# Transposed x in three places instead of two, block 2's free half ahead of the first selections, and one indirect gather fewer issued ahead

## The chip, the cores and the metric

The kernel runs on one core of one Trainium2 chip. The metric is the device time of one execution in microseconds (us); lower is better. The core has five engines that run beside each other and meet at semaphores: TensorE (PE: matmuls; PEld: its weight loads), VectorE (DVE), ScalarE (ACT), GpSimd (POOL) and SyncE (SP, which here only issues DMAs). SBUF is the on-chip memory, PSUM the banks that TensorE writes.

## The reference, cut to what matters

Two LoRA layers follow each other on x of shape (64, 32, 512), each with one adapter per batch row, chosen by an id:

```
x = x + (x W^T + bias + (x A[id0]^T) Bw[id0]^T)     # 32 adapters, rank 16
x = x + (x B1[id1]^T) A1[id1]^T                     # 8 adapters, rank 16
```

The products are in float32. The kernel splits each operand into a rounded high part and the remaining low part and adds three products (high-high, high-low, low-high), the list `HALVES` in the code.

## The kernel before, in words

The 2048 rows of x are cut in 16 blocks of 128 rows; a block holds four batches (`NB`), so four adapter ids per layer. Everything is unrolled, and each engine has its order written out by hand.

**Set-up.** TensorE transposes W (`w_fill`), the adapter tables (`bw`, `a0` to `a3`) and the first three blocks of x (`x_fill`, L409). It also multiplies tables with each other (`c1_part`, and fill "g", L478 to L482), so that the second layer can act on the first layer's input. ScalarE copies each PSUM result to SBUF as the high part, VectorE subtracts for the low part. The rows by which the second factor is applied (`by_rank`, 640 rows of 644 floats) are written to DRAM by SP, ending with `row_ends` (L223). After that GpSimd can gather.

**Per block k.**
- `x_turn(k)` (VectorE, from block 3 on) puts the transposed x in PSUM bank 7. `xt_high(k)` (ScalarE) and `xt_low(k)` (VectorE) bring it to `xt`, which has two places, used in turn. `xt_high(k)` waits until block k-2's matmuls have read theirs.
- `select(k, layer)` (ScalarE, L566) copies the four batches' adapters of a layer into the D columns of `wd`, beside the columns of W. There are two sets of D columns, so it waits for block k-2 too (`u_filled`).
- `base(k, chunks, halves)` (TensorE, L383) multiplies x by W, in two halves of the output columns. One half takes the D columns along (384 columns a matmul), the other is free of them (256 columns). Each chunk of 128 inputs is three matmuls per half. For even k, half 0 is the free one; for odd k, half 1.
- `turn_u(k)`, `own_u(k)` (VectorE) mask the adapters' output per batch and add one gathered column; `add_gh(k)` (TensorE, L429) adds what the second layer needs of the first layer's update, from `g_sel`, which GpSimd makes in `g_select(k)` from the gathered rows; `u_high(k)` and `u_low(k)` bring that to SBUF.
- `gather(k)` (GpSimd, L316) issues the indirect DMA of 128 rows by id into one of four buffers. `up_high(k)` (ScalarE) and `up_low(k)` (GpSimd) split them in high and low. `up(k)` (TensorE, L435) applies them; `finish(k)` (VectorE) adds the bias; SP stores.

**The order around the change.** GpSimd issues gathers 0, 1 and 2, and then repeats: g_select(k), up_low(k), gather(k+3). SP issues the x loads in groups (`X_GROUPS`): group 3 (block 3) and group 4 (blocks 4 and 5) one straight after the other behind `row_ends`; group 5 (blocks 6 and 7) behind the store of block 0.

TensorE goes from set-up into the blocks in this order: the free half of block 1, the transpose of block 2's x, then block 0's other half: the first two chunks without D columns, a wait for the first selections, `down` (L401) for the D columns of these two chunks alone, and the last two chunks with D columns. Then the D half of block 1 and the free half of block 2, add_gh(0), and so on:

```
            base(0, [0, 1], halves=[1], with_d=False, group_check=False)
            wait_d(0)
            down(0, [0, 1])
            base(0, [2, 3], halves=[1], group_check=False)
```

## Time and profile before

| | |
|---|---|
| time, median of 3 runs | 98.52 us (98.05 to 98.83) |
| the profiled execution's own time | 97.92 us |
| its span in the profile | 95.8 us (2.1 us lie outside) |
| TensorE busy | 91.5 us, 96% of the span |
| VectorE, ScalarE, GpSimd busy | 68%, 61%, 61% |
| granted TensorE clock | full over the span (mean 0.997) |
| one block, from an add_gh in the chain of waits to the next (44.38 to 48.81 us) | 4.4 us |

The times of the table's first line come from executions without the profiler; all rows below come from the one profiled execution and are times from its span's start. Matmuls overlap, so a duration in a timeline row is longer than what the matmul adds to a row of them; the chain of waits counts each stretch once. An engine's idle time before an instruction stands in square brackets, with what ended it.

### The profile page before, as it was taken

To read this page: it belongs to the slowest core of one execution; us is meant where nothing else is said; L and a number is where in the kernel's file an instruction comes from. 1 tells how busy PE (TensorE), PEld (TensorE's weight loads), DVE (VectorE), ACT (ScalarE), POOL (GpSimd) and SP (SyncE) were. 2 spreads that over 40 slices of the span, in tenths; PEclk is the share of its full clock that TensorE was granted. 3 is DMA by queue.
4 is the path that set the end of the run, shared out by engine and by line. 5 is a ranking of instruction groups with operands and counts; after the bars stand their busy time and mean duration, and the time that the engine had idled before them with its cause. 6 is when DMAs were issued, how large, how long until landed. Compare 5 with 4: busy or idle time off the path is not lost.

```text
span 95.8 us, 2305 instructions
## 1 busy us (share of the span) xinstructions
PE 91.5 (96%) x662; PEld 90.0 (94%) x662; DVE 64.8 (68%) x120; ACT 58.7 (61%) x189; POOL 58.0 (61%) x126
## 2 busy tenths in 40 slices
PE   5999999999999999999999999999999999999980
PEld 5899999999899998999999999999999999999970
DVE  4499799227076468959587877768595868786460
ACT  0074598874588796748494948567584949480210
POOL 6504008850568999999576584959585766808500
PEclk9999999999999999999999999999999999999998
DMA  2999998968896289989996499992836354520205
GB/s 40 312 347 387 374 403 262 281 156 214 215 224 223 53 250 238 310 249 235 203 290 218 70 319 209 238 269 91 228 44 229 34 213 54 200 110 0 110 0 219
DMA packets 16335, 19.45 MB, mean 203 GB/s; under 512 B 1444, under 2 KB 11556, under 8 KB 16164
## 3 DMA queue, kind: packets, MB, share of 16 engines
q1 hardware_dynamic: 15040, 14.04, 50.1%
q0 software_dynamic: 1280, 5.28, 22.1%
q8 instruction: 5, 0.08, 0.4%
q14 instruction: 6, 0.05, 0.3%
q10 hardware_dynamic: 4, 0.00, 0.0%
HBM read 13.47 MB, written 5.84 MB: 202 GB/s over the span
## 4 chain that ended last, share of the span: by engine, by line
PE 90%; DVE 4%; ACT 2%; issue 1%; DVEq 0%; ACTq 0%
PE psum L394 55%; PE psum L440 11%; PE psum L432 4%; PE psum L362 4%; PE psum L480 4%; PE psum L378 4%; PE psum L370 3%; DVE table_rounded L640 3%; PE psum L466 2%; PE psum L414 1%; PE psum L405 1%; PE psum L448 1%; DVE y L679 1%; ACT row_ends L558 1%; ACT table_rounded L558 1%
## 5 line engine op out<-in xcount | busy, mean ns | idle before, releaser
L394 PE MATMUL psum<-wd,xt 128*128 128x256 f32 (+1 forms) x384 | 62.3, 310 | 0.0
L394 PEld LDWEIGHTS psum<-wd,xt 128*128 128x128 f32 x384 | 56.1, 188 | 0.0
L558 ACT ACTIVATE wd<-table_rounded 128x128 fp32r x128 | 27.7, 297 | 14.7 <-PE psum L394 12.5
L339 POOL TENSOR_TENSOR up_rows<-gathered_rows,up_rows 128x512 fp32r<-128x512 f32 x16 | 20.6, 1289 | 14.0 <-ACT up_rows L558 14.0
L322 POOL DMA_INDIRECT gathered_rows<-by_rank,rows x16 | 15.9, 996 | 6.3 <-DMA by_rank<-row_ends 3.8
L640 DVE TENSOR_TENSOR xt<-psum,xt 128x512 fp32r<-128x512 f32 x16 | 11.1, 691 | 6.6 <-ACT xt L558 5.9
L647 DVE STREAM_TRANSPOSE psum<-x_squares 128x512 f32<-128x512 f32 x13 | 14.4, 1110 | 0.0
L440 PE MATMUL psum<-up_rows,u_sel 128*128 128x256 f32 x96 | 14.2, 284 | 0.0
L440 PEld LDWEIGHTS psum<-up_rows,u_sel 128*128 128x128 f32 x96 | 12.8, 190 | 0.2
L659 DVE STREAM_TRANSPOSE psum<-psum 128x128 f32<-128x128 f32 x16 | 5.3, 330 | 11.2 <-PE psum L394 7.8
L332 POOL TENSOR_TENSOR g_sel<-gathered_rows,batch_mask 128x16 f32<-128x16 f32 x64 | 12.1, 227 | 0.9 <-DMA gathered_rows<-by_rank,rows 0.7
L558 ACT ACTIVATE xt<-psum 128x512 fp32r<-128x512 f32 x16 | 9.6, 597 | 4.4 <-DVE psum L647 1.8
L679 DVE TENSOR_TENSOR y<-psum,bias_all 128x512 f32<-128x512 f32 x15 | 10.4, 692 | 1.1 <-PE psum L440 0.5
L558 ACT ACTIVATE up_rows<-gathered_rows 128x512 fp32r<-128x512 f32 x16 | 10.0, 623 | 0.0
L558 ACT ACTIVATE u_sel<-psum 128x128 fp32r<-128x128 f32 x16 | 4.2, 262 | 5.8 <-PE psum L432 5.8
L432 PE MATMUL psum<-u_own,g_sel 128*128 128x128 f32 x32 | 6.3, 279 | 0.1
L640 DVE TENSOR_TENSOR u_sel<-psum,u_sel 128x128 fp32r<-128x128 f32 x16 | 4.6, 288 | 2.3 <-ACT u_sel L558 2.3
L666 DVE SCALAR_TENSOR_TENSOR u_own<-psum,gathered_rows,batch_mask 128x128 f32<-128x128 f32 x16 | 5.6, 348 | 0.5
L432 PEld LDWEIGHTS psum<-u_own,g_sel 128*128 128x128 f32 x32 | 5.3, 188 | 0.5 <-issue 0.5
L281 POOL COPY a_by_rank<-a_rows 128x1024 f32<-128x1024 f32 x1 | 2.0, 2010 | 5.3 <-DMA a_rows<-in_L_cond_A 5.3
L362 PE MATMUL psum<-warm 128*128 128x128 f32 x16 | 3.9, 425 | 1.1 <-DVE warm L683 1.1
L362 PEld LDWEIGHTS psum<-warm 128*128 128x128 f32 x16 | 3.6, 330 | 1.1 <-DVE warm L683 1.1
(60 smaller groups left out, 72.1 us busy)
## 6 DMA issues: line engine op xcount, KB each, us to landing
out<-y SPq DMA_DIRECT2D x15, 256.0 KB
x_squares<-in_x SPq DMA_DIRECT2D x8, 256.0 KB
w_rows<-in_L_cond_base_weight SPq DMA_DIRECT2D x4, 256.0 KB, 4.0
bw_rows<-in_L_cond_lora_B_w SPq DMA_DIRECT2D x1, 1024.0 KB, 7.0
a_rows<-in_L_cond_lora_A_w SPq DMA_DIRECT2D x1, 1024.0 KB, 9.2
by_rank<-bw_by_rank SPq DMA_DIRECT2D x4, 256.0 KB
x_squares<-in_x SPq DMA_DIRECT2D x8, 128.0 KB
x_rows<-in_x SPq DMA_DIRECT2D x3, 256.0 KB, 9.3
```

Of the source, the lines that this page charges most:

```text
L322: nc.gpsimd.indirect_dma_start(out=gathered_rows[:, k % GATHERS, :], out_offset=None, in_=by_rank_dram[:, :], in_offset=bass.IndirectOffse ...
L332: last = nc.gpsimd.tensor_tensor(out=g_sel[:, k % 2, b, L1, :], in0=gathered_rows[:, k % GATHERS, bass.ds(n1[b] * R + G_COL, R)], in1=batc ...
L339: nc.gpsimd.tensor_tensor(out=up_rows[:, k % 2, LO, :], in0=gathered_rows[:, k % GATHERS, 0:D], in1=up_rows[:, k % 2, HI, :], op=ALU.subtr ...
L362: nc.tensor.matmul(XT[:, 0:P], warm[:, :], warm[:, :], start=True, stop=True)
L394: last = nc.tensor.matmul(bank_of(k, half)[:, start:end], xt[:, k % 2, c, x_part, :], wd[:, w_part, c, col:col + end - start], start=(c == ...
L432: nc.tensor.matmul(u_now, g_sel[:, k % 2, :, :, :], u_own[:, :], start=True, stop=True).then_inc(gh_filled, 1)
L440: last = nc.tensor.matmul(products(k)[:, half, :], u_sel[:, k % 2, u_part, :], up_rows[:, k % 2, r_part, half * HALF:(half + 1) * HALF], s ...
L558: return nc.scalar.activation(dst, src, ACT.Copy)
L640: return nc.vector.tensor_tensor(out=dst, in0=whole, in1=high, op=ALU.subtract)
L647: nc.vector.transpose(out=XT.rearrange("p (c b s) -> p b c s", c=C, b=NB), in_=x_squares[:, k * NB:(k + 1) * NB, :].rearrange("p b (i c) - ...
L666: nc.vector.scalar_tensor_tensor(out=u_own[:, :], in0=u_blocks, scalar=gathered_rows[:, k % GATHERS, BB_COL:BB_COL + 1], in1=batch_mask[:, ...
L679: nc.vector.tensor_tensor(out=y[:, k % SLOTS, :].rearrange("p (h n) -> p h n", h=2), in0=products(k), in1=bias_all[:, :].rearrange("p (h n ...
```

## The change

- `xt` gets three places (`X_SLOTS`). `xt_high(k)` then waits for block k-3.
- The transpose of block 2's x stands straight behind the table product "g" on TensorE, ahead of the 16 transposes of the `a` table. `xt_high(2)` moves ahead of the four `table0` copies on ScalarE, `xt_low(2)` ahead of the four `table0` subtractions on VectorE.
- TensorE does the free half of block 2 straight behind that of block 1, then waits for the first selections, then does the whole D half of block 0 in one piece. `down` and the form of `base` without D columns go.
- ScalarE: `up_high(0)` stands ahead of `select(2, L1)`, `xt_high(3)` behind `u_high(0)`. `select` loads its ids ahead of its wait.
- VectorE: `own_u(0)` stands ahead of `x_turn(3)`.
- GpSimd: gathers 0 and 1 are issued ahead, and then gather(k+2) behind up_low(k).
- SP: the load of x group 4 waits until gather 0 has landed.

```
+X_SLOTS = 3
+ROWS_AHEAD = 2
-        xt = sb("xt", [P, 2, C, 2, P], F32R)
+        xt = sb("xt", [P, X_SLOTS, C, 2, P], F32R)
@@ SP
             for k in range(NBLK - 1):
+                if k == 0:
+
+                    sp.wait_ge(gathered[0], 16)
                 if k in (0, 1, 3, 6):
                     load_x(4 + (0, 1, 3, 6).index(k))
@@ GpSimd
-            gather(0)
-            gather(1)
-            gather(2)
+            for k in range(ROWS_AHEAD):
+                gather(k)
             for k in range(NBLK):
                 g_select(k)
                 up_low(k)
-                if k + 3 < NBLK:
-                    gather(k + 3)
+                if k + ROWS_AHEAD < NBLK:
+                    gather(k + ROWS_AHEAD)
@@ TensorE
             last.then_inc(filled, 1)
+            x_fill(2)
             pe.wait_ge(a_in, 16)
...
             base(1, range(C), halves=[1])
-            x_fill(2)
+            wait_x(2)
+            wait_drained(pe, "a0")
+            base(2, range(C), halves=[0])
+
+
             wait_drained(pe, "c1")
-            base(0, [0, 1], halves=[1], with_d=False, group_check=False)
             wait_d(0)
-            down(0, [0, 1])
-            base(0, [2, 3], halves=[1], group_check=False)
+            base(0, range(C), halves=[1])
             wait_drained(pe, "a3")
             wait_d(1)
             base(1, range(C), halves=[0])
-            wait_x(2)
-            base(2, range(C), halves=[0])
             add_gh(0)
@@ ScalarE
+                if k >= X_SLOTS:
+                    act.wait_ge(u_filled, k - X_SLOTS + 1)
+                copy(xt[:, k % X_SLOTS, :, HI, :], chunked(XT)).then_inc(xt_hi_ready, 1)
...
+            xt_high(2)
             for g in range(4):
...
-            xt_high(2)
             select(2, L0)
+            up_high(0)
             select(2, L1)
-            up_high(0)
+            u_high(0)
             xt_high(3)
-            u_high(0)
             select(3, L0)
@@ VectorE
+            xt_low(2)
             for g in range(4):
...
             turn_u(0)
-            xt_low(2)
+            own_u(0)
             x_turn(3)
-            own_u(0)
+            u_low(0)
             xt_low(3)
-            u_low(0)
             turn_u(1)
```

TensorE's instructions before, from the table product "g" (L480) to the second add_gh (L432). The L394 rows are `base`, L405 is `down`, L414 the transpose of block 2's x, L440 `up`:

```order
L480 MATMUL psum<-b_cols,bw_cols 128x128 x16
L487 MATMUL psum<-ident,a_rows 128x128 x16
L394 MATMUL psum<-wd,xt 128x256 x12
L414 MATMUL psum<-ident,x_rows 128x128 x4
L394 MATMUL psum<-wd,xt 128x256 x6
L405 MATMUL psum<-wd,xt 128x128 x6
L394 MATMUL psum<-wd,xt 128x384 x18
L394 MATMUL psum<-wd,xt 128x256 x12
L432 MATMUL psum<-u_own,g_sel 128x128
L394 MATMUL psum<-wd,xt 128x384 x6
L440 MATMUL psum<-up_rows,u_sel 128x256 x6
L394 MATMUL psum<-wd,xt 128x384 x6
```

The same stretch after the change (L397 is `base` now, L408 the transpose, L426 add_gh, L434 `up`):

```order
L474 MATMUL psum<-b_cols,bw_cols 128x128 x16
L408 MATMUL psum<-ident,x_rows 128x128 x4
L482 MATMUL psum<-ident,a_rows 128x128 x16
L397 MATMUL psum<-wd,xt 128x256 x24
L397 MATMUL psum<-wd,xt 128x384 x24
L426 MATMUL psum<-u_own,g_sel 128x128
L397 MATMUL psum<-wd,xt 128x384 x6
L434 MATMUL psum<-up_rows,u_sel 128x256 x6
L397 MATMUL psum<-wd,xt 128x384 x6
L426 MATMUL psum<-u_own,g_sel 128x128
```

The four transposes moved up by 28 matmuls, the six matmuls of 128 columns are gone, and six of 256 columns became six of 384. The 24 of 256 columns all stand ahead of the first one that needs a selection.

ScalarE before, from the last copy of select(2, L0) on: the ids' load and four copies of select(2, L1), up_high(0), xt_high(3), u_high(0), and the ids' load of select(3, L0):

```order
L241 TENSOR_LOAD ids
L558 ISA
L558 ACTIVATE wd<-table_rounded 128x8x16
L558 ISA
L558 ACTIVATE wd<-table_rounded 128x8x16
L558 ISA
L558 ACTIVATE wd<-table_rounded 128x8x16
L558 ISA
L558 ACTIVATE wd<-table_rounded 128x8x16
L558 ACTIVATE up_rows<-gathered_rows 128x512
L558 ACTIVATE xt<-psum 128x4x128
L558 ACTIVATE u_sel<-psum 128x128
```

The same stretch after the change:

```order
L553 ACTIVATE up_rows<-gathered_rows 128x512
L246 TENSOR_LOAD ids
L553 ISA
L553 ACTIVATE wd<-table_rounded 128x8x16
L553 ISA
L553 ACTIVATE wd<-table_rounded 128x8x16
L553 ISA
L553 ACTIVATE wd<-table_rounded 128x8x16
L553 ISA
L553 ACTIVATE wd<-table_rounded 128x8x16
L553 ACTIVATE u_sel<-psum 128x128
L553 ACTIVATE xt<-psum 128x4x128
```

up_high(0), which waits for gather 0, now stands ahead of the four copies of select(2, L1), and u_high(0) ahead of xt_high(3).

## Rows read from the trace of the kernel before

**Rows 1.** The page: busy time of each engine, and the chain that ended last.

```profile
PE 91.5 (96%) x662; PEld 90.0 (94%) x662; DVE 64.8 (68%) x120; ACT 58.7 (61%) x189; POOL 58.0 (61%) x126
PE 90%; DVE 4%; ACT 2%; issue 1%; DVEq 0%; ACTq 0%
```

**Rows 2.** The chain of waits in order of time: start us, us, what.

```profile
20.93 2.50 DVE table_rounded L640 x4
...
24.21 0.30 ACT wd L558
...
25.44 4.65 PE psum L394 x30
...
33.17 0.33 PE psum L432 x2
...
36.19 0.46 PE psum L432 x2
...
39.99 0.22 PE psum L432 x2
```

**Rows 3.** Timeline, TensorE: start us, us, engine line operation out<-in xcount [idle before <-releaser].

```profile
21.46 1.68 PE L394 MATMUL psum<-wd,xt 128*128 128x256 f32 x12
22.97 0.65 PE L414 MATMUL psum<-ident,x_rows 128*128 128x128 f32 x4
23.38 0.96 PE L394 MATMUL psum<-wd,xt 128*128 128x256 f32 x6
24.55 0.89 PE L405 MATMUL psum<-wd,xt 128*128 128x128 f32 x6 [0.21 <-ACT wd L558]
25.27 4.81 PE L394 MATMUL psum<-wd,xt 128*128 128x384 f32 x30
```

**Rows 4.** Timeline, ScalarE.

```profile
26.64 0.60 ACT L558 ACTIVATE xt<-psum 128x512 fp32r<-128x512 f32 x1 [1.34 <-issue]
27.14 1.96 ACT L558 ACTIVATE wd<-table_rounded 128x128 fp32r x8
29.00 0.62 ACT L558 ACTIVATE up_rows<-gathered_rows 128x512 fp32r<-128x512 f32 x1
...
32.13 0.90 ACT L558 ACTIVATE wd<-table_rounded 128x128 fp32r x4
```

**Rows 5.** Timeline, GpSimd: gathers 0, 3 and 4, and what stands between them.

```profile
24.63 1.16 POOL L322 DMA_INDIRECT gathered_rows<-by_rank,rows  x1 [3.77 <-DMA by_rank<-row_ends]
...
28.96 0.77 POOL L332 TENSOR_TENSOR g_sel<-gathered_rows,batch_mask 128x16 f32<-128x16 f32 x4 [0.66 <-DMA gathered_rows<-by_rank,rows]
29.69 1.29 POOL L339 TENSOR_TENSOR up_rows<-gathered_rows,up_rows 128x512 fp32r<-128x512 f32 x1
...
31.13 0.99 POOL L322 DMA_INDIRECT gathered_rows<-by_rank,rows  x1
...
34.28 0.99 POOL L322 DMA_INDIRECT gathered_rows<-by_rank,rows  x1 [0.16 <-POOL up_rows L339]
...
38.45 0.75 POOL L332 TENSOR_TENSOR g_sel<-gathered_rows,batch_mask 128x16 f32<-128x16 f32 x4
```

**Rows 6.** DMA queues, 31.0 to 34.5 us: packets, MB, share of 16 engines (q0: gathers).

```profile
q0 software_dynamic: 81, 0.33, 34.1%
```

**Rows 7.** DMA queues, 35.0 to 39.1 us (q1: what SP issues, q0: gathers).

```profile
q1 hardware_dynamic: 1089, 0.60, 60.1%
q0 software_dynamic: 79, 0.33, 35.5%
```

**Rows 8.** DMA queues, 35.0 to 37.25 us.

```profile
q1 hardware_dynamic: 794, 0.40, 75.4%
q0 software_dynamic: 13, 0.07, 31.3%
```

**Rows 9.** Timeline, SP: the store of block 0, then x group 5.

```profile
32.87 0.36 SPq L230 DMA_DIRECT2D out<-y  x1
33.27 2.76 SPq L194 DMA_DIRECT2D x_squares<-in_x  x4
```

More of the change, by code:

```diff
@@ L381, in c1_part, with base @@
                     last.then_inc(filled, 1)
-            def base(k, chunks, with_d=True, halves=range(2), group_check=True):
+            def base(k, chunks, halves=range(2)):
                 left = W_LEFT[k % 2]
                 regions = [(left, left + HALF, P), (left, left + HALF, P + HALF)]
-                if with_d:
-                    at_half, at = U_AT[k % 2]
-                    start = min(at, left)
-                    regions[at_half] = (start, start + HALF + P, min(D_AT[k % 2], P + at_half * HALF))
+                at_half, at = U_AT[k % 2]
+                start = min(at, left)
+                regions[at_half] = (start, start + HALF + P, min(D_AT[k % 2], P + at_half * HALF))
                 for c in chunks:
@@ L393, in base @@
                             start, end, col = regions[half]
-                            last = nc.tensor.matmul(bank_of(k, half)[:, start:end], xt[:, k % 2, c, x_part, :],
+                            last = nc.tensor.matmul(bank_of(k, half)[:, start:end], xt[:, k % X_SLOTS, c, x_part, :],
                                                     wd[:, w_part, c, col:col + end - start],
-                                                    start=(c == 0 and n == 0), stop=(c == C - 1 and n == 2),
-                                                    skip_group_check=not group_check)
-                if with_d and C - 1 in chunks and U_AT[k % 2][0] in halves:
+                                                    start=(c == 0 and n == 0), stop=(c == C - 1 and n == 2))
+                if C - 1 in chunks and U_AT[k % 2][0] in halves:
                     last.then_inc(u_filled, 1)
-            def down(k, chunks):
-                half, at = U_AT[k % 2]
-                for c in chunks:
-                    for x_part, d_part in HALVES:
-                        nc.tensor.matmul(bank_of(k, half)[:, at:at + P], xt[:, k % 2, c, x_part, :],
-                                         wd[:, d_part, c, D_AT[k % 2]:D_AT[k % 2] + P],
-                                         start=False, stop=True, skip_group_check=True)
             def x_fill(k):
@@ L561, in xt_high, with select @@
                 act.wait_ge(xt_filled, k + 1)
+                if k >= X_SLOTS:
+                    act.wait_ge(u_filled, k - X_SLOTS + 1)
+                copy(xt[:, k % X_SLOTS, :, HI, :], chunked(XT)).then_inc(xt_hi_ready, 1)
+            def select(k, layer, n=None):
+                ready, table = ((sel0_ready, table0_rounded), (sel1_ready, table1_rounded))[layer]
+                n = n or adapters_of(act, k, layer)
                 if k >= 2:
                     act.wait_ge(u_filled, k - 1)
-                copy(xt[:, k % 2, :, HI, :], chunked(XT)).then_inc(xt_hi_ready, 1)
-            def select(k, layer, n=None):
-                ready, table = ((sel0_ready, table0_rounded), (sel1_ready, table1_rounded))[layer]
-                if k >= 2:
-                    act.wait_ge(u_filled, k - 1)
-                n = n or adapters_of(act, k, layer)
                 for b in range(NB):
@@ L652, in xt_low @@
                 dve.wait_ge(xt_hi_ready, k + 1)
-                low(xt[:, k % 2, :, LO, :], chunked(XT), xt[:, k % 2, :, HI, :]).then_inc(xt_lo_ready, 1)
+                low(xt[:, k % X_SLOTS, :, LO, :], chunked(XT), xt[:, k % X_SLOTS, :, HI, :]).then_inc(xt_lo_ready, 1)
             def turn_u(k):
```

## The prediction

> **What bounds the kernel now.** I read the page first. TensorE is busy 96% of the span and makes 90% of the chain that ended last [rows 1]. So only two things can move the time: work that TensorE no longer does, and moments at which it waits. I read the chain in order of time next. From 40 us on it is TensorE alone, in blocks of 4.4 us, and nothing in the change takes an instruction from it there. All that can change lies between 20 and 40 us. There the chain leaves TensorE once: the VectorE's four table subtractions and ScalarE's first selection, which ends at 24.51 us [rows 2]. TensorE's timeline shows the price, 0.21 us idle ahead of the 128-column matmuls [rows 3]. The second limit is hidden in "busy": GpSimd. From the landing of gather 0 (28.96 us) it runs g_select, up_low and gather issue in turns of 34.28 - 31.13 = 3.15 us [rows 5], against 33.17 to 36.19 us between TensorE's second and third add_gh [rows 2]. The two run in step until 36 us. Only at the fourth add_gh (39.99 us) does TensorE come after GpSimd's g_sel (38.45 + 0.75 = 39.20 us) with room to spare [rows 2, 5]. What the change is worth is read at that fourth add_gh, because everything behind it is TensorE's own pace.
>
> **TensorE's own work.** Twelve matmuls of 256 columns start 22.97 - 21.46 = 1.51 us before their successor [rows 3], so 0.126 us each. The 4.65 us of the chain are 18 of 384 columns and 12 of 256 [rows 2], so (4.65 - 1.51) / 18 = 0.174 us for one of 384. The six of 128 columns take 25.27 - 24.55 = 0.72 us [rows 3], 0.12 each: a narrow matmul costs nearly as much as one of 256. Removed are six of those (0.72) and six of 256 (0.76), added are six of 384 (1.04): 0.44 us less. The four transposes take 23.38 - 22.97 = 0.41 us [rows 3] and are only moved, so the free half of block 1 starts at 21.46 + 0.41 = 21.87, and ends at 23.38. Block 2's free half fills the time to 24.89.
>
> **The tables come later.** xt_high(2) and xt_low(2) now stand ahead of the table work. Before, four subtractions take 2.50 us [rows 2], 0.62 for one more of the same size in a row of them. ScalarE's copies are 0.60 [rows 4] and half hidden. So the first selection ends at 24.51 + 0.62 = 25.13 us, and TensorE, ready at 24.89, waits until about 25.17: the old wait of 0.21 stays a wait of about 0.28. Then 24 matmuls of 384 columns take 4.18 us, and TensorE is at add_gh(0) at 29.35, where the chain of before had it at 25.44 + 4.65 = 30.09 [rows 2]. That is 0.74 us gained, if the gathered rows are there.
>
> **The first gather.** It was issued at 24.63 us and its rows were used at 28.96 [rows 5], 4.33 us. Gather 3, issued at 31.13 with next to nothing beside it, had its 80 packets through at about 34.5 [rows 6]. With 0.4 to 0.5 us from last packet to use, that is 3.8 us; the issue itself is 0.99 instead of 1.16 [rows 5]. So the rows of gather 0 should be there at 28.4 to 28.5: 0.5 us gained. Bounds: nothing (28.96), or some 0.8 us if company cost it more than the quiet gather 3 shows. But here ScalarE caps it: up_high(0) stands behind select(2, L0), which can only start when block 0's D half is through at 25.17 + 12 x 0.174 = 27.26, plus 0.33 to the signal's use (before, block 0's last matmul went in by 25.27 + 6 x 0.174 = 26.31 and xt_high(2), which waited for it, began at 26.64 [rows 3, 4]), plus 0.95 (half of the 1.96 us in rows 4): 28.5. Landing earlier than that gains nothing.
>
> A rule that says otherwise: the Trainium skill, "DMA: Bandwidth & Descriptors", section "Anatomy of one DMA", gives a gpsimd-issued DMA about 2.0 us plus bytes by 436 GB/s, which is an estimated 2.8 us for 330 KB. Rows 5 and 6 show about 3.8 alone and 4.33 in company, so the measured numbers stay in the sum; by the page every gather would be early, and the result would be that of the first rival.
>
> **A new wait on ScalarE.** Behind add_gh(0), TensorE does block 2's D half, which needs select(2, L1). Before, that was done at 29.10 [rows 4]. Now it stands behind up_high(0): 28.5 + 0.5 for that copy's turn + 0.9 for the four copies [rows 4] = 29.95. TensorE is through with add_gh(0) at 29.6 and waits 0.4 us. Then 6 x 0.174 = 1.04, up(0) with six of 256 columns 0.76, again 1.04: add_gh(1) at 32.85, 0.3 ahead of the old 33.17 [rows 2]. On GpSimd, up_low(0) ends at 29.07 + 0.1 + 1.29 = 30.5, gather 2 is issued at 30.6, g_select(1) is done at 32.4. On VectorE, x_turn(3) now follows own_u(0), from 28.8 to 29.9, and u_low(0) comes at 30.2, so it costs nothing. add_gh(2) then waits for GpSimd's next turn, 0.45 us ahead of before: 36.19 - 0.45 = 35.75. Gather 2 must be there at 34.9. Issued at 30.6 beside the tail of x group 4 (loaded from 28.4 on), it takes what gather 0 took in like company, 4.33: 34.93. It just fits.
>
> **What is late next: gather 3.** It used to be issued at 31.13, in the quiet; now it is issued behind up_low(1), at 34.28 - 0.45 = 33.8, which is where gather 4 stood. The store of block 0 and x group 5 run from 32.87 to 36.03 [rows 9]. Gather 4 got 13 of its 80 packets by 37.25 us while SP's queue moved 794 [rows 8], and all of them only by 39.1 [rows 7]: 4.8 us from its issue, 5.3 with the landing. Nobody missed it, since g_select(4) comes a turn behind g_select(3), at 41.6. Gather 3 is wanted at 38.45 [rows 5]. I take 5.1 us, between this and the 3.8 us of a quiet one, and near the first, since x group 5 still runs but the store of block 1, a turn later, hardly meets it: there at 38.9. g_select(3) ends 0.77 later and add_gh(3) follows at 39.8 to 39.9, against 39.99 before. Bounds: at 3.8 us it is there at 37.6, no wait, and the whole 0.45 us stays; at 6.0 (an estimate: 5.3 and twice the 0.35 us by which it stands closer behind x group 5 than gather 4 did) it comes at 39.8, and add_gh(3) at 40.7, 0.7 us later than before.
>
> The skill, same page, section "Queues, rings and completion order", has each DMA engine go round robin between queues at packet borders; then a 5 KB gather packet would only wait for one small packet of 512 bytes, and gather 3 would hardly suffer. Rows 8 disagree: 13 gather packets in the time of 794 others. The rows decide.
>
> Later gathers have more room. In the steady stretch a turn is 4.4 us, so from the end of up_low(k) to up_high(k+2), the first use, there are 8.8 - 0.62 - 1.29 - 0.16 = 6.7 us [rows 4, 5], more than 5.3. The third place of xt and the ids' loads ahead of the wait free ScalarE where it isn't late: nothing. x group 4 is issued from 28.4 to 31.2 (2.76 us [rows 9]) and first wanted by x_turn(4), behind finish(1) and so behind up(1), not before 35 us; gather 0, in company, was there 4.3 us from its issue: nothing.
>
> **The sum.** -0.74 at add_gh(0); +0.4 for select(2, L1) leaves -0.3; GpSimd's turn sets -0.45 at add_gh(2); +0.35 for gather 3 leaves -0.1 us. Against the profiled execution's 97.92 us that is 97.8. The median of the runs is 0.60 above that execution, so I forecast 98.4.
>
> **The rivals.**
> - All gathers land in time (gather 3 in about 4 us). For it: rows 6. Against: rows 8. Gain 0.45 us, 98.1.
> - TensorE alone sets the pace: table, selections and gathers all early. The most there is: 0.44 us of work, 0.21 idle and some 0.25 of waits from 30.09 to 36.19 (6.1 us, in which 18 matmuls of 384 columns, 18 of 256 and two add_gh of 0.22 make 5.85): 0.9 us, 97.6. Against: two of the waits are moved, not removed.
> - The other side, gather 0 gains nothing: its 4.33 us are its own, and x group 4 (SP's queue was nearly through when it began) never hurt it. Then up_high(0) is at 29.0 as before, select(2, L1) at 30.5, TensorE waits 0.9 us, gather 3 is issued at 34.28 and lands at 39.5, add_gh(3) at 40.45: +0.5, 99.0.
> - The other side, dearer: gather 3 meets more of x group 5 than gather 4 did, being issued 0.65 instead of 1.0 us behind it. It decides from a landing later than 39.1. At 40.1 it costs 1.0 us, since add_gh(3), and with it ScalarE's selections for block 5 behind up_high(3), all move: 99.5.
>
> **Chances.** The forecast (within 0.3 us of it) 0.42, all gathers in time 0.22, TensorE alone 0.10, gather 0 gains nothing 0.15, gather 3 dearer 0.11. The range 97.7 to 99.2 leaves out most of the second and the last. About 1% (1 us) is what a measurement of this kernel tells from no change: faster 0.12, within 0.77, slower 0.11.
>
> **What would show it.** Right: no 128-column matmuls of `down`; add_gh(0) near 29.4 and a stop of about 0.4 us behind it that ScalarE's wd ends; gather 0 used at 28.4 to 28.5; GpSimd idle for about 0.9 us ahead of g_select(3), with the gather as releaser; add_gh(3) at 39.8 to 39.9; span 95.7. Wrong: gather 3 used at once (then 98.1), gather 0 still at 28.9, a stop of TensorE behind 40 us, or a span off by more than 0.7 us.

## The result, and the profile after

| | before | after |
|---|---|---|
| median of 22 runs | 98.53 us (97.92 to 99.51) | 99.68 us (98.14 to 101.07) |
| the profiled execution's own time | 97.92 us | 100.11 us |
| its span | 95.8 us | 98.0 us |
| a second profiled execution | | 99.14 us, span 97.0 |

The changed kernel is slower: the ratio of the executions that lie within 1.5% of their kernel's fastest is 1.006 [1.0033, 1.0088], which leaves out 11 of the changed kernel's 22 and one of before's, so it understates. The medians of all runs stand at 99.68 / 98.53 = 1.012. The changed kernel's best run, 98.14 us, is a run like before's; its others spread over 3 us where before's spread over 1.6. The forecast was 98.4 us and the range ended at 99.2.

The page's lines on engines and chain, after, against [rows 1]:

```profile
PE 91.9 (94%) x656; PEld 90.2 (92%) x656; DVE 64.8 (66%) x120; ACT 59.4 (61%) x189; POOL 57.9 (59%) x126
PE 59%; DMA 24%; issue 5%; SPq 3%; POOL 3%; DVE 1%; ACT 1%; POOLq 0%; DVEq 0%
```

TensorE has six instructions less and about the busy time that it had. But it makes 59% of the chain where it made 90%; DMA, which doesn't stand among the engines of [rows 1]'s chain, makes 24%. The chain in order of time says which transfers (start us, us, what):

```profile
4.55 9.85 DMA x_rows<-in_x
...
21.00 3.75 DMA by_rank<-row_ends
...
25.62 4.01 DMA gathered_rows<-by_rank,rows
...
35.12 5.48 DMA gathered_rows<-by_rank,rows
...
41.68 0.46 PE psum L426 x2
```

The first, 9.85 us, is the load of the first x in the set-up, and has nothing to do with the blocks. The other three make 13.24 us. Where [rows 2] has VectorE's tables, then TensorE throughout, the chain now runs over the landing of `row_ends`, gather 0 (issued at 25.62 us) and gather 3 (at 35.12 us), and from `row_ends` on comes to TensorE only at the fourth add_gh, 41.68 us. TensorE's timeline, after, against [rows 3]:

```profile
22.43 3.09 PE L397 MATMUL psum<-wd,xt 128*128 128x256 f32 x24
25.84 4.47 PE L397 MATMUL psum<-wd,xt 128*128 128x384 f32 x24 [0.32 <-ACT wd L553]
30.73 0.46 PE L426 MATMUL psum<-u_own,g_sel 128*128 128x128 f32 x2 [0.42 <-POOL g_sel L337]
...
41.68 0.46 PE L426 MATMUL psum<-u_own,g_sel 128*128 128x128 f32 x2 [0.86 <-POOL g_sel L337]
```

`down` is gone, and two stops at add_gh have come, both ended by GpSimd's g_sel. GpSimd's timeline, after, against [rows 5], shows why g_sel is late:

```profile
25.62 1.16 POOL L327 DMA_INDIRECT gathered_rows<-by_rank,rows  x1 [4.25 <-DMA by_rank<-row_ends]
...
29.83 0.76 POOL L337 TENSOR_TENSOR g_sel<-gathered_rows,batch_mask 128x16 f32<-128x16 f32 x4 [1.80 <-DMA gathered_rows<-by_rank,rows]
...
35.12 0.99 POOL L327 DMA_INDIRECT gathered_rows<-by_rank,rows  x1 [0.16 <-issue]
...
40.78 0.76 POOL L337 TENSOR_TENSOR g_sel<-gathered_rows,batch_mask 128x16 f32<-128x16 f32 x4 [1.50 <-DMA gathered_rows<-by_rank,rows]
...
42.93 0.99 POOL L327 DMA_INDIRECT gathered_rows<-by_rank,rows  x1
...
49.77 0.76 POOL L337 TENSOR_TENSOR g_sel<-gathered_rows,batch_mask 128x16 f32<-128x16 f32 x4 [2.68 <-DMA gathered_rows<-by_rank,rows]
```

GpSimd waits 1.50 us for gather 3 and 2.68 us for gather 5 (issued at 42.93). Before, it waited for neither: g_select(3) has no idle time in [rows 5], and g_select(5) none in the same timeline.

**One clock for all profiles.** The same program reaches the blocks some tenths earlier or later: in the changed kernel's profile TensorE stood 0.5 us for the first load of x, in the set-up. So times below are also told from the start of ScalarE's copy into `row_ends` at the end of the table product "g". ScalarE's timeline of before, and then of the changed kernel:

```profile
19.81 0.60 ACT L558 ACTIVATE row_ends<-psum 128x512 f32<-128x512 f32 x1 [0.90 <-PE psum L480]
```

```profile
20.30 0.60 ACT L553 ACTIVATE row_ends<-psum 128x512 f32<-128x512 f32 x1 [0.91 <-PE psum L474]
```

Each figure is the start of a TensorE timeline row less the start of that copy; the last column is the span's end less it.

| from the copy, us | add_gh(0) | add_gh(1) | add_gh(2) | add_gh(3) | add_gh(5) | end |
|---|---|---|---|---|---|---|
| before | 10.11 | 13.22 | 16.38 | 20.02 | 28.83 | 75.99 |
| changed | 10.43 | 13.82 | 16.73 | 21.38 | 30.37 | 77.70 |
| changed, second profile | 10.33 | 13.73 | 16.65 | 20.85 | 30.13 | 77.44 |

The 2.2 us between the two spans are then 0.49 of a late start, which has nothing to do with the blocks, some 0.35 up to the third add_gh, 1.0 more at the fourth, and 0.35 more up to the end. The second profile has no late start: 0.27 at the third, 0.56 more at the fourth, 0.62 behind it.

### The profile page after: what moved, and what is told of

It reads as the page before. It is cut to its first block, busy times and chain, and to the rows that moved or that the text cites. A ratio compares the mean times of both kernels' runs of the same rounds, so it can differ in the third digit from the quotient of the medians.

```text
span 98.0 us, 2293 instructions
## 1 busy us (share of the span) xinstructions
PE 91.9 (94%) x656; PEld 90.2 (92%) x656; DVE 64.8 (66%) x120; ACT 59.4 (61%) x189; POOL 57.9 (59%) x126
## 4 chain that ended last, share of the span: by engine, by line
PE 59%; DMA 24%; issue 5%; SPq 3%; POOL 3%; DVE 1%; ACT 1%; POOLq 0%; DVEq 0%
PE psum L397 43%; DMA x_rows<-in_x 10%; DMA gathered_rows<-by_rank,rows 10%; PE psum L434 9%; DMA by_rank<-row_ends 4%; PE psum L474 4%; PE psum L426 3%; POOL g_sel L337 2%; SPq L202 2%; PE psum L408 1%; POOL up_rows L344 1%; DVE y L674 1%; ACT row_ends L553 1%; SPq L205 0%; SPq L204 0%
## 5 line engine op out<-in xcount | busy, mean ns | idle before, releaser
L397 PE MATMUL psum<-wd,xt 128*128 128x256 f32 (+1 forms) x384 | 62.5, 311 | 0.4 <-ACT wd L553 0.3
L397 PEld LDWEIGHTS psum<-wd,xt 128*128 128x128 f32 x384 | 56.4, 188 | 0.7 <-issue 0.7
L434 PE MATMUL psum<-up_rows,u_sel 128*128 128x256 f32 x96 | 14.1, 283 | 0.0
L434 PEld LDWEIGHTS psum<-up_rows,u_sel 128*128 128x128 f32 x96 | 12.9, 190 | 0.0
L426 PE MATMUL psum<-u_own,g_sel 128*128 128x128 f32 x32 | 6.4, 283 | 1.3 <-POOL g_sel L337 1.3
L426 PEld LDWEIGHTS psum<-u_own,g_sel 128*128 128x128 f32 x32 | 5.2, 188 | 2.1 <-DVE u_own L661 1.8
```

The lines of the kernel that those rows point to most:

```text
L397: last = nc.tensor.matmul(bank_of(k, half)[:, start:end], xt[:, k % X_SLOTS, c, x_part, :], wd[:, w_part, c, col:col + end - start], start ...
L426: nc.tensor.matmul(u_now, g_sel[:, k % 2, :, :, :], u_own[:, :], start=True, stop=True).then_inc(gh_filled, 1)
L434: last = nc.tensor.matmul(products(k)[:, half, :], u_sel[:, k % 2, u_part, :], up_rows[:, k % 2, r_part, half * HALF:(half + 1) * HALF], s ...
```

## The experiments

Theory A, from the two profiles: the loss is gather 3, and behind it gather 5, because two gathers ahead put them beside x groups 5 and 6. Theory B: it is the new order in front (the free half, the table a copy later, up_high(0) early). Theory C: it is SP's wait for gather 0.

### Three ahead in the changed kernel

```
-ROWS_AHEAD = 2
+ROWS_AHEAD = 3
```

> The changed kernel with three gathers issued ahead again (gather(k+3) behind up_low(k)); all else as changed. Theory A (gather 3, now issued where gather 4 was, lands late and holds the fourth add_gh): the stop of TensorE ahead of the fourth add_gh (0.86 us) goes, and the one at the sixth with it; time 1.0 to 2.0 us below the changed kernel, ratio to before 0.993 to 1.000. Theory B (the new order on TensorE and ScalarE between 20 and 32 us is what costs): the time stays at 1.006 or more. Theory C (x group 4, held back until gather 0 has landed, is what meets the gathers): partly better, 1.002 to 1.006.

98.3 us against 98.45, ratio 1.0006 [0.9973, 1.0039]. The loss is gone with this one number, as theory A said. From the copy, add_gh(0) is at 9.95, add_gh(3) at 19.93, the end at 75.90. GpSimd, in this kernel's timeline:

```profile
34.26 0.99 POOL L327 DMA_INDIRECT gathered_rows<-by_rank,rows  x1 [0.16 <-POOL up_rows L344]
...
38.45 0.75 POOL L337 TENSOR_TENSOR g_sel<-gathered_rows,batch_mask 128x16 f32<-128x16 f32 x4
```

These are the rows of before almost to the hundredth [rows 5]. But nothing is gained either.

### The changed kernel without SP's wait

```
             for k in range(NBLK - 1):
-                if k == 0:
-                    sp.wait_ge(gathered[0], 16)
```

> The changed kernel without SP's wait for gather 0 ahead of x group 4. Theory A: gather 3 still lands about 5.5 us behind its issue, since its company is x group 5 and the stores; ratio to before 1.005 to 1.015, as the changed kernel. Theory C: the ratio falls to 1.000 or below. If the wait does what it is for (a quiet first gather), gather 0 is used 0.3 us or more later from its issue than the 4.0 us of the changed kernel.

99.89 us, ratio 1.013 [1.0077, 1.0183]. The wait isn't the loss; theory C falls. Gather 3 took from 35.17 us 5.31 us in the chain, add_gh(3) stands at 20.81.

### Two ahead in the kernel before

```
             gather(1)
-            gather(2)
...
-                if k + 3 < NBLK:
-                    gather(k + 3)
+                if k + 2 < NBLK:
+                    gather(k + 2)
```

> The kernel before with one edit: gathers 0 and 1 ahead, then gather(k+2) behind up_low(k). Theory A: this part alone makes it slower than before, by 0.8 to 2 us, ratio 1.008 to 1.02, with TensorE waiting for g_sel ahead of the fourth add_gh. Theories B and C: within 0.3 us of before, ratio 0.997 to 1.003.

100.18 us, ratio 1.0156 [1.0106, 1.0205]: the largest loss of all, with nothing else changed. The chain of this kernel:

```profile
34.69 5.78 DMA gathered_rows<-by_rank,rows
...
42.80 6.93 DMA gathered_rows<-by_rank,rows
...
50.81 0.46 PE psum L431 x2
```

Gather 3 takes 5.8 us to its first use, gather 5 takes 6.9, and TensorE waits at the fourth and the sixth add_gh (21.33 and 30.59 from the copy). Theory A holds for the cause: two ahead costs 0.6 to 1.6%, in either order of the rest.

### The new order alone

The changed kernel with ROWS_AHEAD = 3 and without SP's wait: both edits above together.

> The changed kernel with both DMA edits undone (three gathers ahead, no wait of SP): only the third place of xt and the new order on TensorE, ScalarE and VectorE remain. Theory A: a gain, ratio 0.993 to 0.999, the 0.45 us of the forecast or less. Theory B: 1.003 or more.

98.4 us, ratio 1.0009 [0.9981, 1.0037]. The order neither costs nor gains that these runs could tell; the expected gain (0.993 to 0.999) didn't come. Theory B falls as a cause of the loss; what became of the 0.44 us of TensorE's work is the question of the next runs. This run and the second differ by ROWS_AHEAD alone, and their intervals lie apart (1.0009 and 1.013).

### Three dummy matmuls, in both orders

Is the order's gain lost because TensorE then only waits longer for gather 0? Three matmuls of zeros stand ahead of add_gh(0), into columns that nobody has written yet and that are written anew later. The first kernel has the new order alone, the second is before:

```
+            for _ in range(3):
+                nc.tensor.matmul(bank_of(2, 1)[:, 0:P], warm[:, :], warm[:, :], start=True, stop=True)
             add_gh(0)
```

> The order-only kernel with three matmuls of zeros, 0.22 us each, put ahead of add_gh(0); their result is overwritten. Theory D' says that TensorE has 0.5 us or more to spare there: the time moves by less than 0.3 us, ratio to before 0.999 to 1.004. If TensorE's work sets the pace: +0.67 us, 1.007.

> The kernel before with the same three matmuls ahead of add_gh(0). There TensorE arrives just as g_sel is ready: the time rises by 0.4 to 0.7 us, ratio 1.004 to 1.008. If it stays within 0.1%, TensorE had room there too, and the place is set by something else.

New order: 98.55 us, 1.0012 [0.9981, 1.0042]. Before: 98.8 us, 1.0023 [0.9994, 1.0052], where 1.004 to 1.008 was expected. Neither is clear of noise, so what follows is read from profiles. TensorE's timeline of the new order with the dummies:

```profile
30.09 0.83 PE L500 MATMUL psum<-warm 128*128 128x128 f32 x6
30.75 0.39 PE L423 MATMUL psum<-u_own,g_sel 128*128 128x128 f32 x2
```

The six rows of the dummies take 30.75 - 30.09 = 0.66 us. In the kernel before, add_gh(0) moves from 10.11 to 10.77, the full 0.66, and add_gh(3) from 20.02 to 20.22: on the way some 0.46 us of more work is swallowed. In the new order the profiles compare less simply, because gather 0's issue moved as well. Against the new order alone (gather 0 issued 5.10 us behind the copy) add_gh(0) goes from 10.32 to 10.51 and add_gh(3) from 20.27 to 20.16, but with the dummies gather 0 was issued at 4.62. Against three ahead in the changed kernel (issued at 4.89) they are 0.56 and 0.23 us later. That the new order swallows more than the old one isn't shown.

What sets the pace is read from GpSimd and TensorE. GpSimd's g_sel(2) and TensorE's add_gh(2) and add_gh(3) in the new order alone:

```profile
35.79 0.76 POOL L334 TENSOR_TENSOR g_sel<-gathered_rows,batch_mask 128x16 f32<-128x16 f32 x4
```

```profile
36.69 0.46 PE L423 MATMUL psum<-u_own,g_sel 128*128 128x128 f32 x2
...
40.34 0.38 PE L423 MATMUL psum<-u_own,g_sel 128*128 128x128 f32 x2
```

add_gh(2) starts 36.69 - 35.79 - 0.76 = 0.14 us behind the end of g_sel(2), and add_gh(3) 3.65 us behind that. It is 0.14 with three ahead in the changed kernel and 0.15 before. So in both orders GpSimd's turns, counted from gather 0's landing, set the third add_gh, and while they do, work taken from TensorE ahead of add_gh(0) can't pay. The next two runs tried to shorten those turns.

### A fourth gather ahead, to free GpSimd's first turn

```
-            for k in range(ROWS_AHEAD):
+            for k in range(GATHERS):
                 gather(k)
...
-                if k + ROWS_AHEAD < NBLK:
+                if k >= 1 and k + ROWS_AHEAD < NBLK:
```

> The new order without the DMA edits (as the order-only run), and all four gathers issued ahead, so that GpSimd's first turn has no gather in it. Theory D (in the order-only run the gain of the new order was lost at GpSimd's turns of 3.15 us from the landing of gather 0): g_select(1) comes 1.1 us sooner behind g_select(0), the second and third add_gh 0.3 to 0.6 us sooner, ratio to before 0.993 to 0.998. Theory E (TensorE's own waits for the selections ate the gain): 0.999 to 1.003.

> The kernel before with all four gathers issued ahead, GpSimd's first turn without a gather. Theory D: TensorE's waits at the second and third add_gh, 0.25 us in all, go: ratio 0.996 to 0.999. If the fourth gather delays g_select(0) by more than 0.4 us: 1.000 or above.

The fences show the edit in the new order; in the kernel before it is the same. The new order: 98.96 us, 1.0039 [1.0008, 1.0071], a small loss where a gain was expected. Before: 98.74 us, 1.0026 [0.9994, 1.0058]. GpSimd in the first of them:

```profile
28.95 0.95 POOL L324 DMA_INDIRECT gathered_rows<-by_rank,rows  x1 [0.30 <-issue]
29.92 0.75 POOL L334 TENSOR_TENSOR g_sel<-gathered_rows,batch_mask 128x16 f32<-128x16 f32 x4
```

The fourth issue ends only when gather 0 has long landed (ScalarE uses it 4.12 us from its issue, GpSimd 4.94), so what the first turn saves, its start loses; add_gh(0) waits 0.96 us for it and add_gh(3) stands at 20.70.

### Filling the wait for gather 0 with block 2's D half

The new order alone; TensorE takes the first two chunks of block 2's D half ahead of add_gh(0), and ScalarE makes their selection ahead of up_high(0):

```
-            add_gh(0)
             wait_d(2)
             base(2, [0, 1], halves=[1])
+            add_gh(0)
+            base(2, [2, 3], halves=[1])
             up(0)
-            base(2, [2, 3], halves=[1])
             add_gh(1)
...
             select(2, L0)
+            select(2, L1)
             up_high(0)
-            select(2, L1)
             u_high(0)
```

> The order-only kernel with block 2's D half put where TensorE waits: its first two chunks ahead of add_gh(0), its last two ahead of up(0), and select(2, L1) ahead of up_high(0) for that. Theory D' (what was gained ahead of add_gh(0) is lost waiting for gather 0, since nothing else may run there): TensorE has work through the wait, ratio to before 0.993 to 0.998. Theory F (ScalarE's selections and copies are then what is late): 0.999 to 1.006, with waits behind ScalarE's up_rows or wd.

99.52 us, 1.01 [1.0056, 1.0144]: 1% lost, more than either theory had. ScalarE and then GpSimd, in this kernel's timeline:

```profile
30.42 0.61 ACT L550 ACTIVATE up_rows<-gathered_rows 128x512 fp32r<-128x512 f32 x1
...
31.11 1.28 POOL L341 TENSOR_TENSOR up_rows<-gathered_rows,up_rows 128x512 fp32r<-128x512 f32 x1 [1.07 <-ACT up_rows L550]
```

The selection's place was taken from up_high(0), GpSimd stood idle 1.07 us for it in its first turn, and every later turn came later by that: add_gh(3) at 20.95.

### Only gather 3 late, only the later ones late (before)

```
                 up_low(k)
-                if k + 3 < NBLK:
+                if k == 1:
+                    gather(3)
+                if k >= 1 and k + 3 < NBLK:
                     gather(k + 3)
```

> The kernel before with gather 3 alone issued later: behind up_low(1) with gather 4 right behind it; from then on as before. Theory A in its narrow form (gather 3 alone makes the loss): TensorE waits for g_sel 1 us or more ahead of the fourth add_gh, ratio 1.008 to 1.018, no stop at the sixth. If the later gathers of the two-ahead order make the loss: 0.998 to 1.005.

99.34 us, ratio 1.0086 [1.0058, 1.0113]. But this run doesn't isolate the landing: with gathers 3 and 4 issued one behind the other, GpSimd's turn is longer, and in the profile the stop is at the third add_gh, a turn ahead of gather 3's use:

```profile
37.07 0.46 PE L434 MATMUL psum<-u_own,g_sel 128*128 128x128 f32 x2 [0.90 <-POOL g_sel L332]
```

So its 0.86% bounds nothing of gather 3's transfer alone. The other half:

```
                 up_low(k)
-                if k + 3 < NBLK:
-                    gather(k + 3)
+                if k < 2:
+                    gather(k + 3)
+                if 3 <= k < NBLK - 2:
+                    gather(k + 2)
```

> The kernel before with gathers 3 and 4 issued as before and the later ones as after the change: none behind up_low(2), then gather(k+2) behind up_low(k) from k = 3 on. Theory A in two parts (gather 3 makes 0.85 us of the two-ahead order's 1.5, the gathers beside x group 6 the rest): ratio 1.003 to 1.009, with GpSimd or TensorE waiting for gather 5 ahead of the sixth add_gh. If only gather 3 counts: 0.998 to 1.002.

98.64 us, ratio 1.0022 [0.9993, 1.0052]. GpSimd waits 1.58 us at 46.91 and 2.35 us at 52.40 for gathers, and no add_gh of TensorE waits (28.85 from the copy at the sixth, as before). So here late gathers in the steady stretch cost nothing that can be measured. In the kernels with two ahead, which come there behind a late gather 3, the profiles show 0.1 to 0.5 us lost from the fourth to the sixth add_gh; that the debt makes the difference isn't shown by a run of its own.

### x group 5 one block later

The direct test of theory A's mechanism: two gathers ahead stay, and only the company of gather 3 goes.

```
-                if k in (0, 1, 3, 6):
-                    load_x(4 + (0, 1, 3, 6).index(k))
+                if k in (0, 2, 3, 6):
+                    load_x(4 + (0, 2, 3, 6).index(k))
```

> The changed kernel with x group 5 (blocks 6 and 7) issued behind the store of block 1 instead of block 0. Theory A1 (gather 3 is late because of its company, x group 5 and the stores): gather 3 is used about 4.2 us behind its issue instead of 5.5, no wait of TensorE ahead of the fourth add_gh, ratio to before 0.998 to 1.004. Theory A2 (a gather behind others takes 5.5 us whatever is beside it): 5.3 us or more again and 1.008 to 1.015.

> The run with x group 5 later once more, for a second profile. Its first profile showed gather 3 quiet (used within 4.2 us) and gather 5 at 7.4 us, and a time of 98.3, while other executions took 99.2 to 101.0. Theory A1: in a profile of a longer execution the difference is a stop of TensorE of 1 us or more at the fifth to seventh add_gh, behind a gather beside x group 6.

Six runs: 99.74 us (98.29 to 100.99), ratio 1.0122 [1.0072, 1.0171], where 0.998 to 1.004 was expected; the three fastest alone stand at 1.006. The profile was that of the fastest of them, 98.29 us. A second profile has 100.08 us. In both, gather 3 is out of the way. GpSimd and the queues in the first:

```profile
33.99 0.99 POOL L327 DMA_INDIRECT gathered_rows<-by_rank,rows  x1 [0.15 <-issue]
...
38.18 0.75 POOL L337 TENSOR_TENSOR g_sel<-gathered_rows,batch_mask 128x16 f32<-128x16 f32 x4
```

DMA queues, same kernel, 34.0 to 37.4 us (packets, MB, share of 16 engines):

```profile
q0 software_dynamic: 84, 0.33, 35.6%
q1 hardware_dynamic: 160, 0.29, 22.7%
```

No wait ahead of g_select(3), and add_gh(3) at 19.81 from the copy, and at 19.80 in the second profile: the only kernels that beat before's 20.02 there by as much as 0.2. Then gather 5 meets x group 6, which holds four blocks where group 5 holds two. The second profile's chain, and its queues from 41.3 to 49.7 us:

```profile
41.34 8.33 DMA gathered_rows<-by_rank,rows
...
50.75 0.46 PE psum L426 x2
```

```profile
q1 hardware_dynamic: 2915, 1.64, 94.9%
q0 software_dynamic: 87, 0.33, 19.3%
```

In the fastest run gather 5 took 7.42 us in the chain and cost TensorE 0.3 us; in the second profile 8.33 and 1.2 us, a stop of the size that was expected there. So the same program differs from run to run by how gather and x load meet. That isn't all of the 1.8 us between the two spans (96.2 and 98.0), though: 1.04 of them is the start (the copy at 19.74 and at 20.78), and 0.76 lies behind it.

### Both x groups a block later

```
-                if k in (0, 1, 3, 6):
-                    load_x(4 + (0, 1, 3, 6).index(k))
+                if k in (0, 2, 4, 6):
+                    load_x(4 + (0, 2, 4, 6).index(k))
```

> The changed kernel with x group 5 issued behind the store of block 1 and x group 6 behind that of block 3 (before: blocks 0 and 2). Theory A1 (two gathers ahead fail because gathers 3 and 5 meet x groups 5 and 6): gathers 3 and 5 are used 4 to 5 us behind their issue, TensorE doesn't stop at the fourth or sixth add_gh, ratio to before 0.999 to 1.004. Theory A3 (moving the loads only moves the meeting to another gather): 1.008 or more, with a stop at another add_gh.

98.82 us (97.59 to 99.94), before 98.58, ratio 0.9991 [0.9948, 1.0034]; the medians of all runs stand at 1.002. Two ahead, and the loss is no longer to be seen. The queues while gather 3 is on its way, 35.25 to 38.5 us, and then GpSimd from gather 5 on:

```profile
q0 software_dynamic: 82, 0.33, 34.8%
q1 hardware_dynamic: 135, 0.24, 19.8%
```

```profile
41.67 0.99 POOL L327 DMA_INDIRECT gathered_rows<-by_rank,rows  x1 [0.16 <-POOL up_rows L344]
...
46.52 0.75 POOL L337 TENSOR_TENSOR g_sel<-gathered_rows,batch_mask 128x16 f32<-128x16 f32 x4
```

Neither gather is waited for. GpSimd now waits for gather 4 instead (0.68 us) and for gather 7 (1.61 us), but no add_gh behind the first one stops. (In this profile add_gh(3) is at 20.98 and the end at 76.98 all the same: gather 0 was issued 5.88 us behind the copy, 1.06 later than before, and add_gh(0) stands at 10.79. So the profile shows where the waits went, and the runs that the loss went.) So the cost of two ahead is the company that SP gives the gathers, and not the distance by itself.

### Three ahead and both groups later

The same with ROWS_AHEAD = 3, to see whether the two together beat before.

> The changed kernel with three gathers ahead and x groups 5 and 6 a block later each: both cures at once. Theory A1: with three ahead the gathers had room enough beside the loads, so the second cure adds nothing: ratio to before 0.997 to 1.002. If loads beside gathers cost something even with three ahead: 0.993 to 0.997, a version better than both.

99.75 us, ratio 1.0074 [1.0032, 1.0116], and 1.013 by the medians of all runs: neither of the two outcomes that were expected. At the sixth add_gh it is the earliest of all profiles (28.71 from the copy), and then VectorE waits for x group 6 itself, block 8's transpose:

```profile
55.31 1.10 DVE L642 STREAM_TRANSPOSE psum<-x_squares 128x512 f32<-128x512 f32 x1 [1.64 <-DMA x_squares<-in_x]
```

From the seventh add_gh to the eighth it is 58.83 - 53.64 = 5.19 us for before's 4.43, and these 0.76 us are the whole of what this profile's end, 76.65, lies behind that of three ahead alone, 75.90. Behind the store of block 3 the x load had too little room: it is issued from 45.29 us on and used at 55.31. With two ahead it was issued from 45.74 and used at 54.05 without a wait. Why the load took longer here I can't say; the intervals (to 1.0034 there, from 1.0032 here) just touch.

### The changed kernel, a second profile

> The changed kernel once more, for a second profile. Theory A: whatever its time, the distance from the end of the table product to the fourth add_gh goes with gather 3: 21.6 us in the first profile, with gather 3 used 5.5 us behind its issue; if it is used within 4.8 us this time, the distance is under 20.9.

99.14 us, 1 us less than the first profile. Its chain:

```profile
34.30 5.03 DMA gathered_rows<-by_rank,rows
...
41.66 6.94 DMA gathered_rows<-by_rank,rows
...
49.69 0.46 PE psum L426 x2
```

Gather 3 takes 5.03 us here (5.48 in the first), more than the 4.8 us that the expectation set as its condition, and add_gh(3) is at 20.85 (21.38); gather 5 takes 6.94 and comes into the chain at the sixth add_gh. Of the 1.0 us between the two spans, 0.74 is the start (19.56 for 20.30) and only 0.26 lies behind the copy. But both lose 1.45 to 1.7 us there against before, so the loss is no matter of one unlucky profile.

## Why the prediction was wrong, point by point

**What TensorE does: right.** The rows of 128 columns are gone. From the first matmul of 384 columns to add_gh(0), where nothing is waited for between them (group 5 one block later), it is 9.85 - 5.55 = 4.30 us from the copy's clock, for a forecast of 4.18.

**The tables come later: right, and 0.18 us short.** First selection's matmuls expected 25.17 - 19.81 = 5.36 us behind the copy; 5.54 and 5.55 in the profiles of the changed kernel, and 5.54 to 5.63 in all others with the new order whose row shows it. The stop was 0.32 us for the forecast's 0.28.

**"The rows of gather 0 should be there at 28.4 to 28.5: 0.5 us gained": wrong, and the first step that failed.** That is 8.69 us behind the copy for up_high(0). It was at 9.35 and 9.25 in the changed kernel, 9.19 before. SP's wait did keep x group 4 away from gather 0. DMA queues after, 25.6 to 29.6 us:

```profile
q0 software_dynamic: 95, 0.41, 46.9%
```

Nothing but gather 0 and the first packets of gather 1 moves, and yet g_sel starts 4.21 us behind the issue (3.98 in the second profile) for 4.33 before. Over all profiles it is 3.98 to 4.21 with SP's wait (seven, mean 4.09) and 4.00 to 4.39 without (nine, mean 4.22; the two with four issues ahead are left out, since there GpSimd itself is late). The quiet is worth 0.1 us, not 0.5. I had read 3.8 off gather 3 by its last packet [rows 6]. For gather 3 that is right: in the two kernels with x group 5 a block later and little beside it, ScalarE used it without a wait 3.75 and 3.72 us behind its issue. But gather 0's issue takes 1.16 us where gather 3's takes 0.99, which the prediction names and doesn't add, and gather 1 follows it: some 4 us in all. Besides, gather 0 was issued 5.32 and 5.44 us behind the copy instead of 4.82. That lies in the landing of `row_ends`, and it isn't the change's: the same code up to there had 4.69 (twice), 4.77, 4.89 and 5.88 in the other profiles. What sets it stays open. And where gather 0 was early, up_high(0) never came before 8.96, the same within 0.01 in five profiles: that looks like ScalarE's turn, the cap that the prediction named and put at 8.69 (an argument, not tested).

So add_gh(0) stood at 10.43 and 10.33 from the copy instead of 9.54, and add_gh(2), which should have been 0.45 us earlier than before, came 0.35 and 0.27 later. That is the rival "gather 0 gains nothing". In the kernel without SP's wait, where gather 0 was issued at 4.74 and nothing was late in front, it came out in pure form: add_gh(2) at 16.44 for before's 16.38, and add_gh(3) 0.79 us later than before, where that rival had 0.5.

**"A new wait on ScalarE" of 0.4 us: right in kind.** From add_gh(0) to the next row it is 31.22 - 30.73 = 0.49 us, of which add_gh itself takes 0.22: 0.27 lost.

**"What is late next: gather 3": right in place and mechanism; the sum failed by its start.** I had its issue at 33.8, 13.99 behind the copy, and 5.1 us to its use. It was issued at 14.82 (35.12) and 14.74 (second profile, 34.30): 0.8 us later, of which 0.6 to 0.7 come from gather 0's rows. From issue to first use it took 5.5 and 5.05 us, and 5.8 and 5.3 in the two other kernels with two ahead: the 5.1 was 0.3 short on average. Together they make add_gh(3) 21.38 and 20.85 where the forecast had 39.85 - 19.81 = 20.04. The chances were given as if "gather 0 gains nothing" (0.15) and "gather 3 dearer" (0.11) were apart. They add up: the first moves gather 3's issue, the second its landing. In the first profile both came; in the second the landing took the forecast's 5.1 and only the issue was late.

**"Later gathers have more room ... 6.7 us, more than 5.3": wrong.** Gather 5 took 6.84 us to g_sel (42.93 to 49.77), 6.9 to its first use in the second profile and in the kernel before with two ahead, 7.4 and 8.3 with x group 5 moved; without SP's wait it was 6.2. I had priced the company from gather 4's meeting with x group 5 and didn't ask what gather 5 meets: x group 6, of four blocks instead of two, whose load stands behind the store of block 2. With it falls the sentence that everything behind the fourth add_gh is TensorE's own pace: 0.35 and 0.62 us of the changed kernel's loss lie there. From the fourth to the sixth add_gh it is 8.81 us before (48.64 - 39.83), and 8.99 and 9.28 in the changed kernel: 0.2 to 0.5 us more. In the dearest case, group 5 a block later, second profile, it is 10.17.

The waits of the changed kernel (engine, line, releaser: us in all, times, longest) sum it up: gathers are waited for five times by GpSimd and five times by ScalarE, and two of these waits, for gather 0 and for gather 3, reach TensorE through g_sel (the last line).

```profile
POOL g_sel L337 <- DMA gathered_rows<-by_rank,rows: 8.0, 5, 2.7
ACT up_rows L553 <- DMA gathered_rows<-by_rank,rows: 5.2, 5, 2.0
PE psum L426 <- POOL g_sel L337: 1.3, 2, 0.9
```

What runs show: three ahead and all else as changed, 1.0006; two ahead, in either order, 1.006 to 1.016; two ahead with both x groups out of the way, 0.9991 [0.9948, 1.0034]. By the medians of all runs these are 0.998, 1.012 to 1.018, and 1.002. How the loss divides between gathers 3 and 5 is read from profiles alone: in the four with two ahead and the x groups in their places, the fourth add_gh loses 0.56 to 1.3 us on the third, and the sixth 0.1 to 0.5 on the fourth. The attempt to part them by runs failed for gather 3, as told.

**The queues.** From 36.0 to 38.0 us of the changed kernel, while gather 3 is under way and x group 5 loads:

```profile
q1 hardware_dynamic: 681, 0.34, 62.9%
q0 software_dynamic: 20, 0.10, 25.6%
```

20 gather packets beside 681 others looks like [rows 8] again. But both readings leave out when a gather's packets can come at all. In the quiet case, gather 0 after, the first one moved 1.8 us behind the issue, for gather 3 before it was 1.6. Gather 3 was issued at 35.12, so most of the 681 passed at a distance from the issue at which even a quiet gather has none or few. DMA queues after, first 36.12 to 37.12 us and then 37.12 to 38.62 us:

```profile
q1 hardware_dynamic: 554, 0.28, 98.2%
```

```profile
q0 software_dynamic: 54, 0.26, 67.0%
q1 hardware_dynamic: 138, 0.07, 16.9%
```

And the quiet gather 0, 27.12 to 28.62 us (1.5 to 3.0 us behind its issue, where the rows of gather 3 are from 2.0 to 3.5 us):

```profile
q0 software_dynamic: 52, 0.26, 73.6%
```

Once its packets came, gather 3 moved as many in 1.5 us as the quiet gather did, beside 138 others. What it lost is 0.2 to 0.4 us ahead of its first packet (2.0 us behind the issue) and about 1 us in its last 26: they were through 4.6 us behind the issue, for 3.4 in the quiet. Gather 5 lost more in front: its first packet moved 3.0 us behind its issue, and 984 of SP's had moved in the 2 us before it. By the rule of the Trainium skill, "DMA: Bandwidth & Descriptors", section "Queues, rings and completion order", that engines go round robin between queues at packet borders, the prediction reckoned that gather 3 would hardly suffer. It did suffer. But whether that goes against the rule can't be told here: these rows don't show when a gather's packets stood ready, nor how many of the profile's small packets make up one of the page's. "Rows 8 disagree" said more than rows 8 show.

**The spread.** Before, no gather is in the chain; in each profile of the changed kernel two are. That the 98.1 to 101.1 us of the changed kernel come from how gathers and x loads meet is likely, and not shown: only two of its executions were profiled, and they differ more by their start than by their gathers. The kernel with group 5 one block later bears out a part of it: between its two profiles (98.29 and 100.08 us) the sixth add_gh moves from 29.10 to 29.97 from the copy with gather 5, but more of the difference, 1.04 us, is the start.

## What to carry to other kernels

When a prefetch distance is cut, list for every later transfer what it will now run beside, and not only for the first; each periodic load on another queue is a separate meeting, and the room has to cover the worst of them. Before counting work that is taken from the bounding engine, put dummy work of the same size there: if a few blocks on little has moved, the saving won't show either. And tell the times of two profiles from a common event near the change, since the start alone moved by 1.2 us here.

## What the runs showed of the hardware that was not expected

- An indirect gather of 128 rows and 0.33 MB was there within 3.72 and 3.75 us of its issue with little beside it (gather 3, used without a wait, x group 5 a block later), 4.0 to 4.4 us as the first of two or three (gather 0), 5.0 to 5.8 us beside x group 5, and 6.2 to 8.3 us beside x group 6, which is twice as large. In the longest case the 16 DMA engines were busy 94.9% with SP's queue.
- Much of what company costs such a gather can lie ahead of its first packet: that moved 1.6 to 1.8 us behind the issue in the quiet, and 3.0 us behind it for gather 5 of the changed kernel.
- The landing of `row_ends` let gather 0 be issued 4.6 to 5.9 us behind the copy in executions of the same or nearly the same code. Nothing in the profiles tells why.
- The start of the blocks, by the copy into `row_ends`, lay anywhere from 19.56 to 20.78 us over all profiles, though no instruction ahead of it differs: 1.2 us, three quarters of before's whole spread. It goes with the first load of x: in the six profiles whose list of waits has no stop of TensorE for it the copy is at 19.56 to 19.92, and in the four with a stop of 1.1 to 1.4 us at 20.49 to 20.78.
